# Routing logits from float16 halves, and the projection's bias added to the residual rows

## The chip, the cores and the metric

The kernel runs on one core of one Trainium2 chip. Its time is that of one execution on the device in microseconds; the median of three runs stands below. The engines are TensorE (PE in the profile, PEld for its weight loads), VectorE (DVE), ScalarE (ACT), GpSimd (POOL) and SyncE (SP, which here only issues DMAs).

## The reference

Cross-attention with tanh gate, then a mixture of experts with top-2 routing on the normalized rows, all in float32:

```python
def _L0_xattn_ref(q, k, v, w_qs, w_ks, w_vs, w_proj, b_proj):
    qh = jnp.einsum('bld,hdk->hblk', q, w_qs)
    kh = jnp.einsum('bld,hdk->hblk', k, w_ks)
    vh = jnp.einsum('bld,hdk->hblk', v, w_vs)
    attn = jax.nn.softmax(jnp.einsum('hblk,hbmk->hblm', qh, kh), axis=-1)
    out = jnp.einsum('hblm,hbmk->hblk', attn, vh) * qh
    out = out.transpose(1, 2, 0, 3).reshape(q.shape[0], q.shape[1], -1)
    return out @ w_proj.T + b_proj

def _L0_ffn_ref(x, gate_w, w1, w2):
    logits = jnp.einsum('td,ed->te', xt, gate_w)
    w_topk, sel = jax.lax.top_k(logits, K)
    w_topk = jax.nn.softmax(w_topk.astype(jnp.float32), axis=-1).astype(x.dtype)
    ...
    h = jax.nn.silu(jnp.einsum('td,edf->tef', xt, w1))
    y = jnp.einsum('tef,efd->ted', h, w2)
    out = jnp.einsum('ted,te->td', y, combine)

x = x + jnp.tanh(g_xattn[0]) * _L0_xattn_ref(_layernorm(x, axis=-1), ctx_1024, ctx_1024, ...)
x = x + jnp.tanh(g_ffn[0]) * _L0_ffn_ref(_layernorm(x, axis=-1), L0_ffn_gate_w, L0_ffn_w1, L0_ffn_w2)
```

x is 4 x 1024 rows of 256. There are 16 heads of 64, a context of 64 rows a batch, 8 experts with 1024 hidden columns, and K is 2. The bias b_proj is drawn with a spread of 0.1, so it is not zero.

## The kernel before

The kernel has two stages. `attention` (to about 380 us of the span) makes the attention, its residual sum, the routing, and writes each row twice, as a record per chosen expert, to DRAM. `experts` (the rest) works through 71 blocks of 128 records, with two products a block (L1372 and L1385), and adds the weighed results to the output.

Attention takes the 4096 rows in 8 groups of 512 (`NG`, `G`), a group as 4 tiles of 128 rows (`TG`). A group has 8 steps, one for each pair of heads (`p`). All engines run the same 64 steps and then a tail of 6, each in its own order written out by hand in a function `step`. They meet only through semaphores. A pair is worked on in a pipeline that is six steps deep: query product (L563), scores (L573) one step later, maximum and subtraction on DVE (L970, L975), exponent on ACT (L790), sum and reciprocal on DVE (L981, L984), the product with the reciprocal on POOL (`pn`, L1180), transposes on PE (L583), the product with v (L593), the product with q on DVE (`times_q`, r, L990), the rounding to float16 on ACT (`r_h`, L796), the rest on POOL (`r_l`, L1186), and the output product on PE (L608, L614), which sums over the eight pairs in the PSUM tile `pair_ps`. Products with a float32 meaning are made of three float16 products: high by high, high by low, low by high. A "high" half is the rounded value, a "low" half what the rounding left.

Other work is laid into fixed steps. In group g:
- step 1 and 2: the normalized rows of group g - 2 (in `rec`) are transposed by PE into `job_ps` in two halves (L622), and ACT copies each half to `x2t` in float32 (L802). In ACT's order the first copy is the first thing of step 2, right behind r_h of step 1; the second stands behind q's copy of step 2. Then PE makes the routing logits in float32 (`logits_products`, L161): 4 tiles by 2 halves of 128 with 8 columns each, which the trace shows as 16 instructions.
- step 3 and 4: DVE chooses the two experts of each row (`choose`, L188 to L201), in small instructions of 32 elements a partition, in a chain where each waits for the one before.
- step 4: PE makes the positions from the masks (`position_products`, 14 float16 products with 8 columns); step 5: DVE makes the record slots (`place`, L208 to L230), and POOL scatters the records, one a step.
- step 1 to 7: the first layer norm of group g + 1 (L903, L911, L914, L918, L716, L497, L725, L923). POOL makes the inverse root at step 3.
- step 6: DVE adds group g - 1's output product times tanh(g_xattn)/64 to its residual rows, `xres` (L996, `residual`). SP loads these rows from x at the start of their group. The statistics of the second layer norm follow at step 7.
- every step: an eighth of an expert's weights is split into halves by ACT (L830) and DVE (L1022).

The bias is part of the output product. ACT and DVE make `bias_rows`, whose row 0 holds the high half of 64 times the bias and whose row 32 the low half. With the last pair of a group PE multiplies `ones` with it, one product of 256 columns a tile (L611). The last pair of group g runs at step 5 of group g + 1, that of the last group in the tail.

## Time and profile before

| | us |
|---|---|
| median of 3 runs | 809.75 (808.73 to 811.44) |
| the profiled execution | 810.96 |
| its span | 809.2 |
| PE busy | 764.4 (94%) |
| DVE busy | 590.7 (73%) |
| POOL busy | 404.4 (50%) |
| ACT busy | 382.7 (47%) |

The span runs from the first to the last instruction; the execution's time has 1.8 us around it. Busy time is summed over both stages, and the stages differ: a share says little on which engine sets the pace of one of them. A timeline row gives an instruction's start and duration, both in us, and in brackets how long its engine had been idle before it and whom it waited for. An instruction can start before the one ahead of it on its engine has ended, so the distance between two starts is what an instruction costs its engine.

### The profile page before, as it was taken

The numbers are of one execution on the slowest core, as the hardware profiler recorded it, in microseconds if no ns is written. First come the engines' busy times: TensorE is split into PE (matmuls) and PEld (weight loads), VectorE is DVE, ScalarE is ACT, GpSimd is POOL, SyncE is SP. The second block draws the span as 40 slices with busy tenths as digits, with TensorE's granted clock in tenths as the row PEclk, the third lists the DMA queues.
The fourth block names the chain that finished last, engine by engine and source line by source line (L and its number), as shares of the span: only waits on it lengthen the run. The fifth ranks groups of instructions, "written<-read, shape, count | busy, mean of one in ns | idle before, by whom it ended". The sixth has DMA issues, their size and how long they took to land. (4 is left out here: it accounts for less than half of the span.)

```text
span 809.2 us, 22334 instructions
## 1 busy us (share of the span) xinstructions
PE 764.4 (94%) x7778; PEld 643.3 (79%) x7779; DVE 590.7 (73%) x1242; ACT 382.7 (47%) x688; POOL 404.4 (50%) x381
## 2 busy tenths in 40 slices
PE   3989999999999999997899989899999999999993
PEld 1656777777777777775899988899999999999993
DVE  7568798989898989795758668565665665666660
ACT  3565676666667666753345342233333333333230
POOL 5124444766665665664424657544434444444442
PEclk9999999999999999999899999999999999999997
DMA  7404151727263534422787854333233233222321
GB/s 263 183 1 156 45 191 59 261 73 263 77 217 123 186 122 157 158 105 79 235 229 213 240 145 110 62 47 51 47 46 50 46 47 48 49 46 47 52 28 20
DMA packets 48914, 92.61 MB, mean 114 GB/s; under 512 B 4936, under 2 KB 32656, under 8 KB 48848
## 3 DMA queue, kind: packets, MB, share of 16 engines
q1 hardware_dynamic: 25808, 64.84, 23.4%
q0 software_dynamic: 13392, 18.03, 12.8%
q10 hardware_dynamic: 9648, 8.85, 4.3%
q8 instruction: 41, 0.67, 0.4%
q14 instruction: 25, 0.20, 0.1%
HBM read 53.76 MB, written 37.95 MB: 113 GB/s over the span
## 5 line engine op out<-in xcount | busy, mean ns | idle before, releaser
L1372 PE MATMUL h_ps<-bx_h,w_now 128*128 128x128 f16 x2272 | 195.9, 220 | 0.6 <-DVE w_now L1508 0.6
L1385 PE MATMUL pair_ps<-weights,ht_h 128*128 x1136 | 190.3, 273 | 1.3 <-DVE ht_l L1516 0.8
L1372 PE MATMUL h_ps<-bx_l,w_now 128*128 128x128 f16 x1136 | 157.0, 220 | 0.0
L1372 PEld LDWEIGHTS h_ps<-bx_h,w_now 128*128 128x128 f16 x2272 | 154.4, 98 | 2.5 <-issue 1.2
L1385 PE MATMUL pair_ps<-weights,ht_l 128*128 x568 | 154.8, 273 | 0.0
L1444 ACT ACTIVATE hid<-h_ps 128x1024 f32<-128x1024 f32 x71 | 72.7, 1024 | 155.8 <-PE h_ps L1372 149.6
L1615 POOL TENSOR_TENSOR wait_mark<-wait_mark 128x1 f32<-128x1 f32 x71 | 44.6, 629 | 184.1 <-ACT y L1451 135.4
L1616 POOL DMA_INDIRECT out<-y,meta x71 | 124.7, 1757 | 17.9 <-issue 10.5
L1186 POOL TENSOR_TENSOR r_l<-r,r_h 128x512 f16<-128x512 f32 x64 | 74.3, 1161 | 110.9 <-ACT r_h L796 110.5
L1514 DVE CAST ht_h<-hid 128x1024 f16<-128x1024 f32 x71 | 49.5, 698 | 100.9 <-ACT hid L1444 100.3
L1385 PEld LDWEIGHTS pair_ps<-weights,ht_h 128*128 128x128 f16 x1136 | 110.1, 98 | 15.5 <-issue 1.8
L1508 DVE COPY w_now<-weights 128x4096 f16 x71 | 87.3, 1229 | 8.8 <-issue 2.9
L1516 DVE TENSOR_TENSOR ht_l<-hid,ht_h 128x1024 f16<-128x1024 f32 x71 | 87.0, 1226 | 2.4
L1372 PEld LDWEIGHTS h_ps<-bx_l,w_now 128*128 128x128 f16 x1136 | 88.0, 99 | 0.0
L1451 ACT ACTIVATE y<-pair_ps,meta 128x256 f32<-128x256 f32 x71 | 33.7, 474 | 107.5 <-DMA out<-y,meta 63.8
L1180 POOL TENSOR_TENSOR pn<-ex,rinv 128x512 f32<-128x512 f32 x64 | 66.5, 1038 | 35.0 <-DVE rinv L984 35.0
L573 PEld LDWEIGHTS s_ps<-kb,q 128*128 128x128 f32 x512 | 67.9, 193 | 8.6
L573 PE MATMUL s_ps<-kb,q 128*128 128x128 f32 x512 | 68.1, 276 | 0.0
L593 PE MATMUL ot_ps<-e,vb 128*128 128x512 f32 x128 | 65.6, 594 | 0.1
L608 PE MATMUL pair_ps<-wp_h,r_h 128*128 128x256 f16 x256 | 60.7, 273 | 0.1
L608 PE MATMUL pair_ps<-wp_l,r_h 128*128 128x256 f16 x256 | 60.7, 273 | 0.0
L1385 PEld LDWEIGHTS pair_ps<-weights,ht_l 128*128 128x128 f16 x568 | 55.6, 98 | 5.2
(258 smaller groups left out, 1351.8 us busy)
## 6 DMA issues: line engine op xcount, KB each, us to landing
stage<-in_w SPq DMA_DIRECT2D x16, 1024.0 KB, 8.1
w_split<-split SPq DMA_DIRECT2D x14, 1024.0 KB, 5.9
weights<-w_split SPq DMA_DIRECT2D x14, 1024.0 KB
rows<-records ACTq DMA_DIRECT2D x67, 129.0 KB
xin<-in_x SPq DMA_DIRECT2D x8, 512.0 KB, 5.7
x_even<-in_x SPq DMA_DIRECT2D x4, 512.0 KB
x_odd<-in_x SPq DMA_DIRECT2D x4, 512.0 KB
out<-x_even SPq DMA_DIRECT2D x4, 512.0 KB
```

The lines of the kernel that those rows point to most:

```text
L573: last = nc.tensor.matmul(s_ps[:, t].rearrange("p h m -> p (h m)"), q32[:, p, t * P:(t + 1) * P], kb[:, b, p, :] if isinstance(b, int) els ...
L593: nc.tensor.matmul(ot_ps[:, :], vb[:, b, p].rearrange("p h w -> p (h w)"), e32[:, p % 2, :], start=True, stop=True).then_inc(ot_mm, 1)
L608: nc.tensor.matmul(pj_ps[:, t, :], r_h[:, p % 2, t * P:(t + 1) * P], wt[:, p, :], start=(p == 0 and i == 0 and t % 2 == 0), stop=False, sk ...
L1180: nc.gpsimd.tensor_tensor(pn[:, p % 2].rearrange("p t (h m) -> p t h m", h=2), ex[:, p % 2].rearrange("p t (h m) -> p t h m", h=2), rinv[: ...
L1186: nc.gpsimd.tensor_tensor(r_l[:, p % 2, :], r32[:, p % 2, :], r_h[:, p % 2, :], ALU.subtract).then_inc(r_lo, 1)
L1372: last = nc.tensor.matmul(h_ps[r % 2][:, c, :], w1_now[:, r % 2, s, k * F + c * P:k * F + c * P + P], xt[:, r % 2, k, :], start=(j == 0 an ...
L1385: last = nc.tensor.matmul(y_ps[r % 2], ht[:, r % 2, c, :], weights_at(e, s, WN // 2 + c * D, D).rearrange("p o n -> p (o n)"), start=(c == ...
L1444: nc.scalar.activation(hid[:, r % 2], h_ps[r % 2][:, :, :], ACT.Silu, scale=1.0 / WS).then_inc(h_act, 1)
L1508: nc.vector.tensor_copy(w1_now[:, r % 2], weights[:, bass.ds(e, 1), :, 0:KD * F].rearrange("p o s n -> p (o s) n")).then_inc(w1_ready, 1)
L1514: nc.vector.tensor_copy(ht_h[:, r % 2], hid[:, r % 2]).then_inc(h_hi, 1)
L1516: nc.vector.tensor_tensor(ht_l[:, r % 2], hid[:, r % 2], ht_h[:, r % 2], ALU.subtract).then_inc(h_lo, 1)
L1616: pool.indirect_dma_start(out, bass.IndirectOffsetOnAxis(meta[:, r, 0:1].bitcast(U32), 0), y[:, r % 2, :], None, compute_op=ALU.add).then_ ...
```

## The change

The routing's normalized rows are kept as float16 halves instead of float32. ACT's two copies write the high halves. DVE gets a function `x2_split` that subtracts them from the PSUM tile and writes the low halves; it stands at steps 1 and 2, behind `times_q` and ahead of the expert split. The gate's weights are split once, in the setup. The logits are 24 products (4 tiles, 3 pairs of halves, 2 halves of the columns). PE's second transposes and its logits wait for DVE's subtractions (`x2_low`), where they waited for ACT's copies. The last two groups are routed in the expert stage, by the code as it was.

The bias leaves the output product. DVE makes tanh(g_xattn) times the bias once, in `tbias`, on all 128 partitions. POOL adds it to the residual rows in place (`add_bias`), 1024 elements a partition: for group g - 1 at the start of step 4 of group g, ahead of pn, and for the last group in the tail ahead of its fourth step. DVE's `residual` waits for POOL's sum in place of the load.

```diff
--- before.py
+++ after.py
+        carry.gate_hl = carried("gate_hl", [P, 2, KD, E], F16)
...
-    bias_rows = sb("bias_rows", [P, D], F16)
-    bias_high = sb("bias_high", [64, D], F16)
+    tbias = sb("tbias", [P, D], F32)
...
-    bias_sb = sb("bias_sb", [64, D], F32)
+    bias_sb = sb("bias_sb", [P, D], F32)
...
+    x2t_hl = x2t[:, :, :].rearrange("p k n -> p (k n)").bitcast(F16).rearrange("p (s k n) -> p s k n", s=2, k=KD)
...
+    biased = sem("biased")
+    gate_split, x2_low = sem("gate_split"), sem("x2_low")
...
-        sp.dma_start(bias_sb[:, :], dram["bproj"].partition_broadcast(64)).then_inc(bias_in, 16)
+        sp.dma_start(bias_sb[:, :], dram["bproj"].partition_broadcast(P)).then_inc(bias_in, 16)
...
-                pe.wait_ge(bias_hi, 2)
-                pe.wait_ge(bias_lo, 1)
...
@@ -607,8 +607,6 @@
 
                     nc.tensor.matmul(pj_ps[:, t, :], r_h[:, p % 2, t * P:(t + 1) * P], wt[:, p, :],
                                      start=(p == 0 and i == 0 and t % 2 == 0), stop=False, skip_group_check=True)
-                if p == NP - 1:
-                    nc.tensor.matmul(pj_ps[:, t, :], ones[:, :], bias_rows[:, :], start=False, stop=False, skip_group_check=True)
             pe.wait_ge(r_lo, n + 1)
...
         def logits(g):
-            pe.wait_ge(x2_copied, 2 * g + 2)
-            logits_products(nc, job_ps, x2t, gate_t).then_inc(routed.lg_mm, 1)
+            pe.wait_ge(x2_low, 2 * g + 2)
+            if g == 0:
+                pe.wait_ge(gate_split, 2)
+            for t in range(TG):
+                for i, (xs, gs) in enumerate(((0, 0), (0, 1), (1, 0))):
+                    for k in range(KD):
+                        last = nc.tensor.matmul(job_ps[:, t * E:(t + 1) * E], x2t_hl[:, xs, k, t * P:(t + 1) * P], carry.gate_hl[:, gs, k, :],
+                                                start=(i == 0 and k == 0), stop=(i == 2 and k == KD - 1))
+            last.then_inc(routed.lg_mm, 1)
...
             if p == 2 and known(g, 2):
-                pe.wait_ge(x2_copied, 2 * g - 3)
+                pe.wait_ge(x2_low, 2 * g - 3)
                 x2_transpose(g - 2, k, 1)
...
-        act.wait_ge(bias_in, 16)
-        nc.scalar.mul(bias_high[:, :], bias_sb[:, :], WS).then_inc(bias_hi, 1)
-        act.wait_ge(bias_zeroed, 1)
-        nc.scalar.mul(bias_rows[0:1, :], bias_sb[0:1, :], WS).then_inc(bias_hi, 1)
+        act.wait_ge(gate_copied, 1)
+        nc.scalar.copy(carry.gate_hl[:, 0], gate_t[:, :, :]).then_inc(gate_split, 1)
...
@@ -799,7 +802,7 @@
             act.wait_ge(x2_tp, 2 * g + k + 1)
             if k == 0:
                 after(act, routed.lg_mm, g)
-            nc.scalar.copy(x2t[:, k, :], job_ps[:, :]).then_inc(x2_copied, 1)
+            nc.scalar.copy(x2t_hl[:, 0, k, :], job_ps[:, :]).then_inc(x2_copied, 1)
...
-        nc.vector.memset(bias_rows[:, :].bitcast(U32), 0).then_inc(bias_zeroed, 1)
...
-        dve.wait_ge(bias_hi, 1)
-        dve.wait_ge(bias_zeroed, 1)
-        nc.vector.scalar_tensor_tensor(bias_rows[32:33, :], bias_sb[32:33, :], WS, bias_high[32:33, :],
-                                       ALU.mult, ALU.subtract).then_inc(bias_lo, 1)
+        dve.wait_ge(gate_split, 1)
+        nc.vector.tensor_tensor(carry.gate_hl[:, 1], gate_t[:, :, :], carry.gate_hl[:, 0], ALU.subtract).then_inc(gate_split, 1)
...
+        def x2_split(g, k):
+
+            dve.wait_ge(x2_copied, 2 * g + k + 1)
+            nc.vector.tensor_tensor(x2t_hl[:, 1, k, :], job_ps[:, :], x2t_hl[:, 0, k, :], ALU.subtract).then_inc(x2_low, 1)
...
         def residual(g, par):
 
             dve.wait_ge(pj_mm, pair_no(g, NP))
-            dve.wait_ge(xres_in[par], 16 * (g // 2) + 16 if isinstance(g, int) else g)
+            dve.wait_ge(biased, g + 1)
             nc.vector.scalar_tensor_tensor(xres[par][:, :, :], pj_ps[:, :, :], gains[:, 0:1], xres[par][:, :, :],
                                            ALU.mult, ALU.add).then_inc(x1_done, 1)
...
             if pairs_back >= 5:
                 times_q(n - 5, (p - 5) % NP)
+            if p in (1, 2) and known(g, 2):
+                x2_split(g - 2, p - 1)
             for i in pieces(g, p):
                 expert_lo(g, i)
...
                 dve.wait_ge(tanh_done, 1)
                 nc.vector.tensor_scalar(gains[:, :], tanhs[:, :], 1.0 / WS, None, ALU.mult).then_inc(setup_ops, 1)
                 dve.wait_ge(setup_ops, 1)
+                dve.wait_ge(bias_in, 16)
+                nc.vector.tensor_scalar(tbias[:, :], bias_sb[:, :], tanhs[:, 0:1], None, ALU.mult).then_inc(setup_ops, 1)
...
+        def add_bias(g, par):
+
+            pool.wait_ge(xres_in[par], 16 * (g // 2) + 16)
+            if g == 0:
+                pool.wait_ge(setup_ops, 2)
+            nc.gpsimd.tensor_tensor(xres[par][:, :, :], xres[par][:, :, :], tbias[:, :].unsqueeze(1).broadcast_to([P, TG, D]),
+                                    ALU.add).then_inc(biased, 1)
+
         def step(g, k, p, pairs_back=LAST):
             n = pair_no(g, p)
+            if p == 4 and known(g, 1):
+                add_bias(g - 1, 1 - k)
             if pairs_back >= 3:
                 normalize(n - 3, (p - 3) % NP)
...
         for p in range(LAST - 1):
+            if p == 3:
+                add_bias(NG - 1, 1)
             if p < 3:
                 normalize(NS + p - 3, NP + p - 3)
             product_lo(NS + p - 5, NP + p - 5)
```

## Rows read from the trace of the kernel before

**Rows 1.** The page, part 1: busy time of TensorE, share of span, instructions.
```profile
PE 764.4 (94%) x7778; PEld 643.3 (79%) x7779; DVE 590.7 (73%) x1242; ACT 382.7 (47%) x688; POOL 404.4 (50%) x381
```

**Rows 2.** Stretches: length, busy time (instructions) of each engine, clock, DMA share, GB/s.
```profile
core 0: us, PE busy (x) PEld busy (x) DVE busy (x) ACT busy (x) POOL busy (x), PEclk, DMA share, GB/s
...
157.50:200.40 42.90, 42.89 (x307) 31.99 (x306) 39.55 (x103) 29.31 (x56) 27.62 (x28) 1.00 0.47 163
```

**Rows 3.** Timeline of DVE, one group: start, duration, instruction, idle before, releaser.
```profile
164.57 0.69 DVE L1022 SCALAR_TENSOR_TENSOR split<-stage,split 128x512 f16<-128x512 f32 x1 [0.16 <-ACT split L830]
...
166.72 0.19 DVE L188 COPY lg<-job_ps 128x32 f32<-128x32 f32 x1 [0.62 <-PE job_ps L161]
...
168.99 0.69 DVE L970 TENSOR_REDUCE smax<-s_ps 128x8 f32<-128x512 f32 x1 [0.73 <-PE s_ps L573]
...
197.71 0.69 DVE L1022 SCALAR_TENSOR_TENSOR split<-stage,split 128x512 f16<-128x512 f32 x1 [0.69 <-ACT split L830]
```

**Rows 4.** Timeline of PE, same group: logits, positions and bias products.
```profile
164.83 1.85 PE L161 MATMUL job_ps<-gate_t,x2t 128*128 128x8 f32 x16
...
166.53 0.59 PE L563 MATMUL q_ps<-xt_h,wq_h 128*128 128x512 f16 x2
...
176.12 0.17 PE L170 MATMUL job_ps<-seen_h,ones 128*128 128x8 f16 x1
...
176.47 0.59 PE L563 MATMUL q_ps<-xt_h,wq_h 128*128 128x512 f16 x2
...
180.17 0.27 PE L611 MATMUL pair_ps<-bias_rows,ones 128*128 128x256 f16 x1
...
180.50 0.27 PE L611 MATMUL pair_ps<-bias_rows,ones 128*128 128x256 f16 x1
```

**Rows 5.** Timeline of DVE, step 6: the subtraction for xt_l and the next start.
```profile
185.23 0.64 DVE L923 TENSOR_TENSOR xt_l<-job_ps,xt_h 128x512 f16<-128x512 f32 x1
185.79 0.68 DVE L970 TENSOR_REDUCE smax<-s_ps 128x8 f32<-128x512 f32 x1
```

**Rows 6.** Timeline of DVE and ACT together, step 1.
```profile
158.84 0.68 DVE L990 TENSOR_TENSOR r<-ot_ps,q 128x512 f32<-128x512 f32 x1
...
159.56 0.62 ACT L796 CAST r_h<-r 128x512 f16<-128x512 f32 x1
...
159.60 0.69 DVE L1022 SCALAR_TENSOR_TENSOR split<-stage,split 128x512 f16<-128x512 f32 x1
...
160.08 0.58 ACT L802 COPY x2t<-job_ps 128x512 f32<-128x512 f32 x1
```

**Rows 7.** Timeline of POOL and DVE together, steps 3 and 4.
```profile
171.74 1.15 POOL L1186 TENSOR_TENSOR r_l<-r,r_h 128x512 f16<-128x512 f32 x1 [2.19 <-ACT r_h L796]
...
172.46 0.45 DVE L918 SCALAR_TENSOR_TENSOR shift<-mv,rstd 128x4 f32<-128x4 f32 x1
...
172.86 1.03 POOL L1180 TENSOR_TENSOR pn<-ex,rinv 128x512 f32<-128x512 f32 x1
...
173.04 0.90 DVE L192 TENSOR_TENSOR cand<-lg,top 128x32 f32<-128x32 f32 x1
```

**Rows 8.** Timeline of DVE and POOL together, step 3.
```profile
165.90 0.20 DVE L984 RECIPROCAL rinv<-esum 128x8 f32<-128x8 f32 x1
...
166.27 1.04 POOL L1180 TENSOR_TENSOR pn<-ex,rinv 128x512 f32<-128x512 f32 x1
...
167.16 0.19 DVE L192 TENSOR_TENSOR cand<-lg,top 128x32 f32<-128x32 f32 x1
```

**Rows 9.** Groups by line and form on POOL: busy time, mean ns, idle before.
```profile
L1194 POOL TENSOR_TENSOR wait_mark<-wait_mark 128x1 f32<-128x1 f32 x6 | 1.2, 195 | 6.7 <-DVE tok_ids L230 6.7
```

**Rows 10.** Timeline of DVE in the last group, step 4.
```profile
344.22 0.31 DVE L192 TENSOR_TENSOR cand<-lg,top 128x32 f32<-128x32 f32 x1
344.57 0.97 DVE L193 SCALAR_TENSOR_TENSOR cand<-cand,iota_e 128x32 f32<-128x32 f32 x1
```

**Rows 11.** Timeline of POOL in the tail.
```profile
376.43 1.16 POOL L1186 TENSOR_TENSOR r_l<-r,r_h 128x512 f16<-128x512 f32 x1 [2.19 <-ACT r_h L796]
```

More of the change, by code:

```diff
@@ L329, in attention @@
         "base_set", "consts_set", "k_zeroed", "v_zeroed", "wk_laid", "setup_ops", "tanh_done"))
-    ctx_tp, ctx_copied, gate_tp, gate_copied, wp_tp, wp_hi, wp_lo, wq_hi, wq_lo, bias_hi = (sem(n) for n in (
-        "ctx_tp", "ctx_copied", "gate_tp", "gate_copied", "wp_tp", "wp_hi", "wp_lo", "wq_hi", "wq_lo", "bias_hi"))
-    bias_zeroed, bias_lo = sem("bias_zeroed"), sem("bias_lo")
+    ctx_tp, ctx_copied, gate_tp, gate_copied, wp_tp, wp_hi, wp_lo, wq_hi, wq_lo = (sem(n) for n in (
+        "ctx_tp", "ctx_copied", "gate_tp", "gate_copied", "wp_tp", "wp_hi", "wp_lo", "wq_hi", "wq_lo"))
+    biased = sem("biased")
+    gate_split, x2_low = sem("gate_split"), sem("x2_low")
     k_mm, k_placed, v_mm, v_placed = (sem(n) for n in ("k_mm", "k_placed", "v_mm", "v_placed"))
```

## The prediction

> **What bounds the kernel now.** I read the page's busy line first: PE is busy for 94% of the span and DVE for 73% [rows 1]. That average hides two stages, so next came the table by stretches of one group, 42.90 us each. In the stretch shown PE is busy for 42.89 of 42.90 us and its clock is fully granted, so PE sets the pace of the attention stage. DVE is busy for 39.55 us, but its instructions start one right behind the other [rows 2]. The timeline of DVE shows how little room it has: in a whole group only four gaps carry a releaser, of 0.16 us (ACT's half of the expert split), 0.62 us (the logits), 0.73 us (the scores) and 0.69 us (again ACT's split) [rows 3]. That is 2.2 us of 42.90, so DVE is a second bound, 2.2 us behind the first. What the change gives to DVE has to fit in there.
>
> **The PE part.** A group's logits are 16 instructions that begin at 164.83 and end with the next product's start at 166.53: 1.70 us. The new form has 24 products of float16 halves with 8 columns. The nearest float16 products of that size are the 14 of the positions, from 176.12 to 176.47, so 0.025 us each and 24 cost 0.60 us [rows 4]. That saves 1.10 us in each of six groups, 6.6 us; the last two groups are routed in the expert stage by the old code. The bias products come one in three, 0.33 us between two of them, so 0.11 us each [rows 4]: four in each of eight groups, 3.5 us. Were PE the bound to the end, the change would win 6.6 + 3.0 us (the eighth group's bias lies in the tail, where the product waits for r_l anyway), 9.6 us. As bounds for a float16 product of 8 columns I take 0.025 and 0.11 us; at the upper end 24 of them cost 2.6 us and the logits lose 0.9 us a group.
>
> **The DVE part, step 1.** DVE gets two subtractions a group, each like the one that makes xt_l: next start 0.56 us after its own [rows 5]. The first stands at step 1 behind the product r (L990). It waits for ACT's copy of x2, and in ACT's order that copy stands behind the rounding of r to r_h, which waits for this same L990. In the trace L990 starts at 158.84 and ends at 159.52, r_h starts at 159.56, the copy at 160.08 and lasts 0.58 us to 160.66 [rows 6]. So the subtraction can't start before 160.70, and the expert split L1022, which started at 159.60, starts at 161.26: 1.66 us later. This wait is new, it comes in each of six groups, and behind it on DVE stand the sum of the exponents, on which POOL's pn hangs, and everything of step 2. PE's transposes of the second half wait for this subtraction too; I cost that at nothing, since PE has the query and score products of step 2 to do first. Bounds of the term: 0.6 us if ACT were far ahead (its order forbids that), 1.7 us as worked out. I take 1.66.
>
> **Step 2 and 3.** I walk DVE's starts against the old ones, both counted from the maximum of step 1, with which the stretch of rows 2 begins (157.5). At step 2 the second subtraction adds 0.56 us and the 0.16 us gap closes: L1022 at 8.87 instead of 7.04. The logits now wait for that subtraction, which ends at 8.95; before, they started at 7.30. PE idles 1.7 us there, has its logits at about 9.6 and gives back what it saved. DVE reads them at 10.3 instead of 9.2, because its own order reaches them only then. Next is a lock. DVE instructions with two inputs in SBUF stand still while POOL's tensor operations run: at step 4 L192 takes 0.90 us instead of 0.19, starting 0.18 us after pn and ending 0.04 us behind it; L918 ends just behind r_l in the same way [rows 7]. At step 3 today L192 starts at 167.16, when pn (166.27 to 167.31) is nearly through, and takes 0.19 us, since the logits came late enough [rows 8]. Changed, the logits are waiting already, so the copy, the maximum and L192 follow at once behind the reciprocal that lets pn start (165.90 in this group), with two starts of 0.22 us in between, and L192 is held until pn ends: 0.8 us more. The 0.73 us gap before the next maximum then closes. Maximum of step 3: 12.67 instead of 11.46, 1.2 us late.
>
> **Step 4: add_bias.** It stands on POOL ahead of pn and waits for nothing that is late (the residual rows land steps earlier), so it starts where pn starts now, right behind r_l. Its size is 1024 elements a partition. A 512-element POOL operation takes 1.04 us (pn) and 1.15 (r_l), one of a single element 0.195 us [rows 7, 9], so twice the part that grows gives 1.9 to 2.1; I take 2.0, with 1.04 (pn as it is) and 2.3 us (r_l twice) as ends. L192 is held to its end, and pn follows back to back. In the last group this case is already in the trace: L192 slips in at the end of r_l and the next instruction, L193, is held 0.97 us by pn [rows 10]. So DVE waits for add_bias and for pn: 2.0 us more, less the 0.2 us that L193 takes anyway. That is 1.9 us; the maximum of step 4 comes at 20.4 instead of 17.3, and DVE is 3.1 us late. PE's positions wait for the masks and idle some 2 us more. If the lock did not bite, this term would be zero, since POOL's idle time hides it (2.19 us before the r_l of this step [rows 7]) and pn is needed one PE step later.
>
> **Steps 5 to 0.** DVE runs here without a gap until ACT's split at step 0, and that gap stays, since ACT's chain starts from DVE's L990 of step 7. So a group's period becomes 42.9 + 3.07 = 45.96 us. PE stands idle for 4.5 us of it.
>
> **A price from a page.** The rows make add_bias 2.0 us [rows 7, 9]. The Trainium skill, page GPSIMD Engine Reference, section 2.1 (Instruction dispatch), gives about 2.5 cycles an element for two inputs, with a clock of 1.2 GHz; an estimate from that page is 1024 x 2.5 cycles = 2.1 us and the fixed 0.2 us: 2.3 us, and the time would be 1.7 us above my forecast.
>
> **The sum.** Group 1 gains its bias products, 0.4 us, for PE still has the pace there. Five periods lie between step 1 of group 2 and step 1 of group 7: 5 x 3.07 = 15.4 us. Group 7 prepares no next group, so DVE has no statistics to make there and waits for PE at steps 1 and 2 today; PE comes into it some 1 us ahead, and by the same walk DVE is 0.5 us early at step 3. Step 4 makes it 1.6 us later (L192 finds a gap there, L193 and the next one are held [rows 10]), and DVE's waits of steps 6 and 7 take back about 0.5: I count +0.5 us. In the tail add_bias runs in front of the last but one r_l, where POOL waits 2.19 us for ACT [rows 11]: hidden, and if longer, 0.1 to 0.3 us. The setup (a bias load twice as wide, one small split, tanh times bias, against two ACT and one DVE instruction removed) I cost at 0, within 0.5: DVE waits for PE in group 1 and takes it up. The expert stage only moves. Sum: -0.4 + 15.4 + 0.5 = +15.4 us. The profiled execution took 810.96 us (809.2 span and 1.8 around it), 1.2 us above the median of the runs: 826.4 for such an execution, 825.2 against the median. I forecast 825 us.
>
> **Rivals.** (1) PE keeps the pace and the win shows: 809.75 - 9.6 = 800 us. For it speaks PE's 42.89 us; against it DVE's 2.2 us of room, of which the first wait alone takes 1.66. (2) The locks don't add up: add_bias is short for DVE, or L192 gets in first. Then step 3 ends 0.6 us late and ACT's gap at step 0 takes a little: 0.5 us a group, 5 x 0.5 - 0.4 = +2, 812 us. Against it stand 0.90 and 0.97 us in the rows. (3) DVE loses more: add_bias at 2.3 us and L1022, which also has two SBUF inputs, now meeting r_l of POOL at step 1 or 2 for up to 0.4 us each. That is 0.7 to 1 us a group, 5 x 0.9 = 4.5: 830 us. It decides from the point where r_l starts before L1022 ends.
>
> **Chances.** Forecast (820 to 829) 0.60, between it and rival 2 (locks in part) 0.13, rival 2 0.10, rival 3 0.08, rival 1 0.09. So the range of 8 in 10 is 811 to 831. About 0.3%, 2.4 us, is what a measurement can tell. Faster by more: rival 1, 0.09. Within: 0.05, the lower part of rival 2. Slower: 0.86.
>
> **What would show it.** In the changed profile a group's period is 46 us and DVE has no gap for scores or logits; a gap of some 1.2 us stands before the x2 subtraction of step 1, released by ACT's copy; the logits' product waits for DVE, the positions for the mask; PE is busy about 41.4 us of 46 (42.9 less 1.1 and 0.4). L192 takes some 2 us at step 4 and L193 1 us, and 1 us at step 3. I am wrong if L192 stays short while add_bias runs, if add_bias is under 1.5 us, or if the period is below 43.

## The result, and the profile after

The changed kernel takes 827.97 us (median of 4 runs, 825.25 to 828.93) and the kernel before, on the same chip, 809.24 us (4 runs, 807.85 to 811.44): a ratio of 1.0223, with a 95% interval of 1.0189 to 1.0258. It is slower, by 18.7 us. The profiled execution took 828.93 us, its span is 827.2 us against 809.2.

Where the 18.0 us of span lie, read from starts of the same instruction in both timelines (after less before):

| stretch | before | after | added |
|---|---|---|---|
| to the maximum of step 1 of group 2 | 114.63 | 115.85 | +1.22 |
| from there to step 1 of group 7 | 213.50 | 231.35 | +17.85 |
| from there to the tail's maximum (group 7) | 35.91 | 36.82 | +0.91 |
| from there to the last attention product | 15.66 | 16.68 | +1.02 |
| from there to the end | 429.5 | 426.5 | -3.0 |

Almost all of it is in the five periods of the attention stage: 46.27 us each instead of 42.70 (in the middle of the stage, 42.90). The last row is the expert stage, which the change doesn't touch. From its last copy of the logits to the end of the span, where all kernels of this document have the same code, the profiled executions took 345.9 to 352.8 us (350.2 before, 348.8 after), so 3 us there are no effect that can be told from that spread.

The page of the kernel after, parts 1 and 2, answers to [rows 1]:

```profile
span 827.2 us, 22385 instructions
## 1 busy us (share of the span) xinstructions
PE 766.9 (93%) x7794; PEld 636.0 (77%) x7795; DVE 615.6 (74%) x1254; ACT 379.9 (46%) x687; POOL 426.9 (52%) x389
...
PEclk9989999999999999999899999999999999999998
```

Three whole periods after, cut where DVE copies the logits, and three slices of 2 us, each just behind a group's logits (length; busy time and count of PE, PEld, DVE, ACT and POOL; granted clock; DMA share; GB/s). They answer to [rows 2]:

```profile
173.02:218.82 45.80, 42.47 (x312) 30.10 (x311) 43.13 (x106) 28.98 (x54) 30.29 (x29) 1.00 0.44 150
218.82:265.70 46.88, 44.10 (x312) 31.37 (x311) 43.11 (x105) 28.93 (x54) 30.28 (x29) 0.96 0.42 147
265.70:311.51 45.81, 42.46 (x310) 30.05 (x309) 43.14 (x105) 28.97 (x54) 30.30 (x29) 0.99 0.43 150
...
219.00:221.00 2.00, 2.00 (x8) 1.46 (x7) 1.83 (x6) 0.60 (x1) 2.00 (x3) 0.50 0.72 193
...
266.00:268.00 2.00, 2.00 (x16) 1.71 (x14) 1.79 (x7) 0.75 (x2) 1.98 (x2) 1.00 0.75 256
...
312.00:314.00 2.00, 2.00 (x8) 1.36 (x7) 1.59 (x5) 0.49 (x1) 1.80 (x3) 0.50 0.76 246
```

PE is no longer busy throughout: 42.5 of 45.8 us, where it was 42.89 of 42.90. DVE has gone from 39.55 to 43.1 us and sets the pace. And there are two kinds of period, 45.8 and 46.9 us; in the longer one the granted clock is 0.96 over the period and 0.50 in the slice just behind the logits. The clock falls behind the first, the third and the fifth of the six logits (from 126, 218 and 311 us). The third of these falls lies in the last period, 45.71 us, which is shorter by itself, since group 7 prepares no next group: without a fall it is 44.50 us (see the spare products).

DVE's timeline of one group after (start, duration, instruction, idle before and what ended it), from two groups of rows, answers to [rows 3, 7, 8]:

```profile
165.88 0.69 DVE L965 TENSOR_TENSOR x2t<-job_ps,x2t 128x512 f16<-128x512 f32 x1 [1.17 <-ACT x2t L805]
...
173.02 0.14 DVE L189 COPY lg<-job_ps 128x32 f32<-128x32 f32 x1
...
173.42 0.92 DVE L193 TENSOR_TENSOR cand<-lg,top 128x32 f32<-128x32 f32 x1
...
179.33 2.21 DVE L193 TENSOR_TENSOR cand<-lg,top 128x32 f32<-128x32 f32 x1
181.58 0.97 DVE L194 SCALAR_TENSOR_TENSOR cand<-cand,iota_e 128x32 f32<-128x32 f32 x1
```

POOL's timeline over the same step, and in the tail (this answers to [rows 7, 11]):

```profile
179.14 2.35 POOL L1213 TENSOR_TENSOR x_even<-x_even,tbias 128x1024 f32<-128x1024 f32 x1
181.46 1.04 POOL L1189 TENSOR_TENSOR pn<-ex,rinv 128x512 f32<-128x512 f32 x1
...
394.17 2.54 POOL L1213 TENSOR_TENSOR x_odd<-x_odd,tbias 128x1024 f32<-128x1024 f32 x1
396.67 1.16 POOL L1195 TENSOR_TENSOR r_l<-r,r_h 128x512 f16<-128x512 f32 x1
```

Read the two together: L193 starts at 179.33, 0.19 us behind the start of add_bias, and ends at 181.54; add_bias ends at 181.49. L194 starts 0.12 us behind pn and ends at 182.55; pn ends at 182.50. A comparison of 32 elements, 0.19 us by itself, ends when the POOL instruction ends under which it started.

PE's timeline: the logits' product of two groups, and the products behind it in the second (answers to [rows 4]):

```profile
171.73 0.76 PE L630 MATMUL job_ps<-gate_hl,x2t 128*128 128x8 f16 x24 [1.54 <-DVE x2t L965]
172.34 0.59 PE L565 MATMUL q_ps<-xt_h,wq_h 128*128 128x512 f16 x2
...
217.52 0.76 PE L630 MATMUL job_ps<-gate_hl,x2t 128*128 128x8 f16 x24 [1.54 <-DVE x2t L965]
218.14 0.59 PE L565 MATMUL q_ps<-xt_h,wq_h 128*128 128x512 f16 x2
218.57 0.82 PE L565 MATMUL q_ps<-xt_l,wq_h 128*128 128x512 f16 x2
219.18 1.06 PE L565 MATMUL q_ps<-xt_h,wq_l 128*128 128x512 f16 x2
220.03 1.91 PE L575 MATMUL s_ps<-kb,q 128*128 128x128 f32 x8
```

The 24 products take 0.61 us (171.73 to 172.34), so they are as cheap as they were to be. But PE now stands 1.54 us in front of them, and in the second group a pair of 512-column products that takes 0.59 us at full clock takes 1.06 behind that wait: the clock is at its lower level, 1.2 instead of 2.4 GHz.

### The profile page after: what moved, and what is told of

Same layout as the page of the kernel before. It is cut to its first block and busy times, and to the rows that moved or that the text cites. A ratio compares the mean times of both kernels' runs of the same rounds, so it can differ in the third digit from the quotient of the medians.

```text
span 827.2 us, 22385 instructions
## 1 busy us (share of the span) xinstructions
PE 766.9 (93%) x7794; PEld 636.0 (77%) x7795; DVE 615.6 (74%) x1254; ACT 379.9 (46%) x687; POOL 426.9 (52%) x389
## 5 line engine op out<-in xcount | busy, mean ns | idle before, releaser
L1465 ACT ACTIVATE hid<-h_ps 128x1024 f32<-128x1024 f32 x71 | 72.7, 1024 | 155.9 <-PE h_ps L1393 148.4
L1636 POOL TENSOR_TENSOR wait_mark<-wait_mark 128x1 f32<-128x1 f32 x71 | 47.9, 675 | 182.5 <-ACT y L1472 134.0
L1637 POOL DMA_INDIRECT out<-y,meta x71 | 121.7, 1714 | 16.5 <-issue 9.1
L1195 POOL TENSOR_TENSOR r_l<-r,r_h 128x512 f16<-128x512 f32 x64 | 76.1, 1190 | 101.3 <-ACT r_h L799 101.3
L1189 POOL TENSOR_TENSOR pn<-ex,rinv 128x512 f32<-128x512 f32 x64 | 66.6, 1040 | 45.1 <-DVE rinv L989 45.1
L575 PEld LDWEIGHTS s_ps<-kb,q 128*128 128x128 f32 x512 | 69.5, 200 | 14.4 <-issue 7.5
L575 PE MATMUL s_ps<-kb,q 128*128 128x128 f32 x512 | 71.3, 284 | 2.7 <-DVE ssub L980 2.7
L799 ACT CAST r_h<-r 128x512 f16<-128x512 f32 x64 | 39.4, 616 | 72.0 <-DVE r L995 71.7
```

What stands on the lines that cost most here:

```text
L575: last = nc.tensor.matmul(s_ps[:, t].rearrange("p h m -> p (h m)"), q32[:, p, t * P:(t + 1) * P], kb[:, b, p, :] if isinstance(b, int) els ...
L1189: nc.gpsimd.tensor_tensor(pn[:, p % 2].rearrange("p t (h m) -> p t h m", h=2), ex[:, p % 2].rearrange("p t (h m) -> p t h m", h=2), rinv[: ...
L1195: nc.gpsimd.tensor_tensor(r_l[:, p % 2, :], r32[:, p % 2, :], r_h[:, p % 2, :], ALU.subtract).then_inc(r_lo, 1)
L1465: nc.scalar.activation(hid[:, r % 2], h_ps[r % 2][:, :, :], ACT.Silu, scale=1.0 / WS).then_inc(h_act, 1)
L1637: pool.indirect_dma_start(out, bass.IndirectOffsetOnAxis(meta[:, r, 0:1].bitcast(U32), 0), y[:, r % 2, :], None, compute_op=ALU.add).then_ ...
```

## The experiments

My theory after the result: the loss is DVE's, in two parts that add up. The bias part costs through the hold of choose()'s two-input instructions by add_bias at step 4; the logits part through the wait for ACT's half at step 1 and the hold at step 3. The rivals: POOL's longer work delays its own results; PE's clock, which falls behind the new wait, is the main part; one of the two edits does nothing. "Period" is the distance between two copies of the logits by DVE (L189 after, L188 before) in the middle of the stage, so the last of the five, shorter in most kernels, is left out; each ratio is to the kernel before, timed on the same chip in the same session.

| kernel | median us | ratio (95% interval) | period us |
|---|---|---|---|
| before | 809.2 to 809.9 | 1 | 42.90 |
| after | 827.97 | 1.0223 (1.0189 to 1.0258) | 45.8 / 46.9 |
| logits only | 815.34 | 1.0071 (1.0039 to 1.0104) | 43.7 / 45.2 |
| bias only | 821.22 | 1.0148 (1.0119 to 1.0176) | 44.69 |
| after, bias at step 6 | 812.80 | 1.0060 (1.0028 to 1.0093) | 43.8 / 45.1 |
| after, half of the bias | 819.79 | 1.0139 (1.0109 to 1.0168) | 44.70 |
| after, choose() through PSUM | 813.65 | 1.0058 (1.0036 to 1.0079) | 43.4 / 45.1 |
| bias only, at step 6 | 808.06 | 0.9989 (0.9957 to 1.0020) | 42.80 |
| step 6 and PSUM | 816.93 | 1.0080 (1.0056 to 1.0105) | 43.4 / 45.1 |
| step 6, PSUM, split later | 804.48 | 0.9938 (0.9911 to 0.9964) | 42.83 |
| after, split later | 824.89 | 1.0201 (1.0165 to 1.0236) | 45.18 |
| step 6, PSUM, spare products | 809.86 | 1.0000 (0.9975 to 1.0025) | 43.44 |
| after, spare products | 824.42 | 1.0179 (1.0143 to 1.0214) | 45.78 |
| step 6, split later | 808.50 | 0.9990 (0.9963 to 1.0017) | 43.16 |

**Logits only.** The kernel before with the float16 logits; the bias stays a product.

> The kernel before with the float16 logits alone; the bias stays in the output product. My theory (the new wait of the logits on ACT's and DVE's halves moves DVE's r = ot*q of step 1, and through it GpSimd's r_l, onto choose()'s two-input instruction of step 3, but nothing is added to the lock of step 4): DVE ends some 1 to 1.3 us late a group, of which the period takes 0.9 to 1.3, so 809.5 + 5 x 1.1 = about 815 (812 to 818), and the lock at step 3 is 0.9 us as in the kernel after. Rival A, GpSimd's add_bias has no part in the loss and the logits alone do it all: 828, with the logits 45.8 us or more apart. Rival B, the products saved on PE pay for the wait: 803 to 806.

Measured: 815.34 us, periods of 43.70 and 45.19 us in turn. The total is the theory's, but partly by luck. The 43.70 is +0.80, just below the 0.9 to 1.3 us that DVE's walk gives; the periods of 45.19 I had not expected, and they are not DVE's: the granted clock is 0.50 behind the logits with which they begin (see the spare products below).

**Bias only.** The kernel before with add_bias at step 4.

> The kernel before with the bias part alone: add_bias of 2.35 us on GpSimd in step 4, the float32 logits as they were. My theory (DVE is held at choose()'s two-input instruction of step 4 by add_bias, about 2.2 us where it was about 0.3 held before, and has some 2.2 us of waits a group to give up before it sets the period, while PE saves 0.11 us at each of four bias products): the period stays within -0.4 to +0.5 us of 42.9, so 807 to 812, with the waits of DVE for PE gone in the rest of the group. Rival, the lock doesn't matter and the period is PE's: 42.9 - 0.44, so 806. Rival 2, both parts simply add and this one is worth 2 us a group: 819.

Measured: 821.22 us, outside my range and nearest to the second rival: the parts nearly add (0.71% and 1.48% make 2.19%, and both together cost 2.23%; by the periods without a fall of the clock, 0.80 and 1.79 us make 2.59, and both together cost 2.90). DVE's timeline of one group:

```profile
168.29 0.19 DVE L188 COPY lg<-job_ps 128x32 f32<-128x32 f32 x1 [0.62 <-PE job_ps L161]
...
170.56 0.69 DVE L956 TENSOR_REDUCE smax<-s_ps 128x8 f32<-128x512 f32 x1 [0.73 <-PE s_ps L572]
...
174.62 2.21 DVE L192 TENSOR_TENSOR cand<-lg,top 128x32 f32<-128x32 f32 x1
176.86 0.97 DVE L193 SCALAR_TENSOR_TENSOR cand<-cand,iota_e 128x32 f32<-128x32 f32 x1
```

The hold is as forecast: L192 and L193 take 3.18 us where they took 1.09 [rows 7], 2.09 more. But the waits of 0.62 and 0.73 us are still there, unchanged. They were never room. DVE's lag of step 4 reaches PE (its positions now wait 0.78 us for the masks, and later scores 0.42 us for DVE), PE comes as much later to the next group's logits, which take it 1.7 us, and DVE waits for them again as before. Only ACT's gap gives something back: 0.86 us a group before, 0.58 now. 2.09 less 0.28 is 1.81, and the period grew by 1.79.

**The bias at step 6.** The same work on POOL at step 6 of the group's own walk: two steps later within the period, and six steps earlier for the group whose rows it is. The call in the tail falls away with it (its removal isn't shown):

```
-            if p == 4 and known(g, 1):
-                add_bias(g - 1, 1 - k)
+            if p == 4 and isinstance(g, int) and g == 1:
+                add_bias(0, 0)
+            if p == 6 and known(g, 1):
+                add_bias(g, k)
```

> The kernel after, but GpSimd adds the bias to a group's rows two steps later, at step 6 of the group's own walk, where DVE has no two-input instruction of choose() in flight. Same work in all. My theory (the place of add_bias, not its length, costs): the 2.2 us hold at step 4 goes to 0.3 or less, some of it comes back where DVE's r = ot*q meets the busy port, and the period falls from 46.3 to 43.7 to 44.5: 812 to 818. Rival, the loss is GpSimd's or PE's clock and not the hold: 826 to 830, unchanged.

> The bias part alone (float32 logits), with add_bias at step 6. The bias part alone at step 4 gave 821 and a period of 44.69 us with every logits wait as before. My theory (the hold on choose() is all of that loss): the 2.21 and 0.97 us instructions go back to 0.90 and 0.19, the period to 42.9 less what PE's saved bias products give, 0 to 0.44: 806 to 810. Rival, GpSimd's longer work delays its r_l or pn and PE with them wherever it stands: 813 or more.

Measured: 812.80 us with both parts and 808.06 with the bias part alone, each inside my range. With the bias part alone the period falls from 44.69 to 42.80 us by the move. In its timelines add_bias is as long as ever, and the two instructions of step 4 are back at the lengths of [rows 7]:

```profile
170.47 0.90 DVE L192 TENSOR_TENSOR cand<-lg,top 128x32 f32<-128x32 f32 x1
171.40 0.19 DVE L193 SCALAR_TENSOR_TENSOR cand<-cand,iota_e 128x32 f32<-128x32 f32 x1
```

```profile
181.99 2.36 POOL L1192 TENSOR_TENSOR x_odd<-x_odd,tbias 128x1024 f32<-128x1024 f32 x1
```

So the place of add_bias cost 1.9 us a group, and its 2.36 us of POOL's time cost nothing. The saved bias products are worth 0.1 us a period (42.80 against 42.90), not 0.44. The rest stays at step 6: PE's transposes of xn begin 0.70 us behind the product ahead of them instead of 0.44, just after ACT has made xn, and take 0.09 us more.

**Half of the bias.** add_bias over half of the tiles; half of the bias is left out.

> The kernel after with add_bias on half of the tiles of each group, 512 elements instead of 1024 in each partition: it leaves half of the bias out. My theory (each microsecond of add_bias is a microsecond of DVE's hold at step 4 and so of the period, since DVE has no room left): the instruction takes 1.18 us, the hold falls by as much, the period by 1.1, and five periods and the tail give 828 - 6 = 822 (820 to 824). Rival, only that an instruction stands there matters, or the clock: 827 to 829.

Measured: 819.79 us, just below the range. The instruction takes 1.26 to 1.31 us, the comparison is held for nearly as long, and the period is 44.70, 1.1 us below the 45.80. The clock falls only once, in its first period (45.77), and three times in the kernel after: over all five periods it is 7.8 us shorter, 5.5 by the hold and the rest by the two falls fewer. DVE and POOL:

```profile
218.85 1.12 DVE L193 TENSOR_TENSOR cand<-lg,top 128x32 f32<-128x32 f32 x1
220.01 0.96 DVE L194 SCALAR_TENSOR_TENSOR cand<-cand,iota_e 128x32 f32<-128x32 f32 x1
```

```profile
L1213 POOL TENSOR_TENSOR x_odd<-x_odd,tbias 128x512 f32<-128x512 f32 x4 | 5.2, 1310 | 0.0
L1213 POOL TENSOR_TENSOR x_even<-x_even,tbias 128x512 f32<-128x512 f32 x4 | 5.0, 1260 | 0.0
```

1.09 us less of hold, 1.1 us less of period: while DVE sets the pace, each microsecond of the hold is one of the period.

**choose() through PSUM.** add_bias stays at step 4, but cand, choice, the second maximum and the copy of the logits that choose() reads lie in unused PSUM columns, so that none of its instructions has two SBUF inputs:

```
+    def spare(i, n=TG * E):
+        return job_ps[:, 128 + 64 * i:128 + 64 * i + n]
...
+        cand, choice, lg = by_tile(spare(0)), spare(1, TG), by_tile(job_ps[:, 0:TG * E])
+        if c:
+            top = spare(2, TG)
...
+        mask = by_tile(spare(3))
+        nc.vector.tensor_tensor(mask, carry.iota_e[:, :, :], over_e(choice), ALU.is_equal)
```

> The kernel after, with add_bias where it is, but choose() keeps cand, choice, the second maximum and the first copy of the logits in spare PSUM columns, so that none of its instructions reads two SBUF operands on DVE (one comparison is done twice for it). My theory (DVE's instructions with two SBUF inputs wait for GpSimd's running tensor_tensor, others don't): the 0.92, 2.22 and 0.97 us instructions of steps 3 and 4 fall to 0.2 each, DVE gets 3.3 us a group back, the period falls from 46.3 to 43 to 43.8 where PE's own work and the logits' wait take over, 809 to 814. Rival A, it is GpSimd's traffic itself that slows any DVE instruction: 828 or worse. Rival B, the hold only moves to the next instruction with two SBUF inputs (split of the expert weights in step 4): about 818 to 822.

Measured: 813.65 us, inside the range. POOL's add_bias still takes 2.35 us and still starts in front of the comparison (174.63 and 174.82), and no instruction of choose() is held. The grouped rows of DVE, all groups (busy us, mean ns, idle before), where L204 and L205 are the comparison and the one behind it:

```profile
L205 DVE SCALAR_TENSOR_TENSOR job_ps<-job_ps,iota_e 128x32 f32<-128x32 f32 x12 | 2.4, 199 | 0.4
...
L204 DVE TENSOR_TENSOR job_ps<-job_ps,top 128x32 f32<-128x32 f32 x6 | 1.2, 200 | 0.2
L204 DVE TENSOR_TENSOR job_ps<-lg,job_ps 128x32 f32<-128x32 f32 x6 | 1.2, 196 | 0.2
```

In the kernel after, the same two have means of 1422 and 689 ns:

```profile
L193 DVE TENSOR_TENSOR cand<-lg,top 128x32 f32<-128x32 f32 x12 | 17.1, 1422 | 0.4
L194 DVE SCALAR_TENSOR_TENSOR cand<-cand,iota_e 128x32 f32<-128x32 f32 x12 | 8.3, 689 | 0.4
```

This shows the mechanism and not only its place: it is the second SBUF operand that makes DVE stand, not POOL's activity. The periods of 45.1 in this kernel, three of the four in the middle, are falls of PE's clock again. The Trainium skill, page SBUF — State Buffer, section "SBUF: two separate sides", says the same: between a DVE instruction with two SBUF inputs and a GpSimd one that reads SBUF, the one that starts first has the port pair for its whole length. The trace agrees: 2.21 us of hold under a 2.35 us instruction, 0.20 us once an operand is in PSUM.

**Both of these.** The kernel after with add_bias at step 6 and choose() through PSUM.

> The kernel after with both: add_bias at step 6 and choose() through PSUM. From the kernel with add_bias at step 6 (812.8, periods 43.8 and 45.1) this takes the last holds of choose(), 0.73 and 0.71 us at steps 3 and 4. If DVE is still the bound, the period falls by 1.1 to 1.4 (one comparison more): 806 to 808. Rival, the half clock that PE falls to behind its logits wait in every second group sets the period: those stay at 45.1 and the time at 812.

Measured: 816.93 us, not 806 to 808, and above the rival's 812 too; the profiled execution took 812.94. Three of its five periods are 45.1 us, as the rival said, the others 43.4 and 42.1; DVE now waits 2.8 to 4.4 us a group and is no bound. What is? In PE's timeline and in slices of 2 us around the logits:

```profile
255.76 0.76 PE L645 MATMUL job_ps<-gate_hl,x2t 128*128 128x8 f16 x24 [1.54 <-DVE x2t L980]
256.38 0.93 PE L580 MATMUL q_ps<-xt_h,wq_h 128*128 128x512 f16 x2
257.10 1.06 PE L580 MATMUL q_ps<-xt_l,wq_h 128*128 128x512 f16 x2
```

```profile
254.00:256.00 2.00, 0.46 (x12) 0.25 (x11) 2.00 (x4) 0.86 (x2) 0.47 (x2) 1.00 0.18 66
256.00:258.00 2.00, 2.00 (x26) 0.98 (x23) 1.83 (x8) 0.70 (x1) 2.00 (x2) 0.62 0.07 20
258.00:260.00 2.00, 2.00 (x9) 1.64 (x8) 0.49 (x3) 0.60 (x1) 1.80 (x3) 0.52 0.93 344
```

PE did 0.46 us of work in the slice ahead, and then its clock is at 0.62 and 0.52. The other groups have the same wait, and behind two of the five the clock stays up.

**Spare products.** To part the clock from the wait: PE runs three products whose result is overwritten, ahead of the wait. Once in that kernel, once in the kernel after.

```
         def logits(g, n, par):
+            after(pe, q_sb, n)
+            for _ in range(3):
+                nc.tensor.matmul(q_ps[1][:, :], wq_h[:, 0, 3 * P:4 * P], xt_h[:, par, 0, :], start=True, stop=True)
             pe.wait_ge(x2_low, 2 * g + 2)
```

> The kernel with add_bias at step 6 and choose() through PSUM (periods 43.4 and 45.1 in turn), and PE runs three spare 128x512 float16 products of about 0.22 us each into the bank that the next q product overwrites, ahead of the logits' wait. Their result is not used. They fill 0.65 of the 1.54 us wait with work and leave what the kernel waits for as it was. My theory (the long periods are PE's clock falling behind that wait): the granted clock stays at 1.00, every period is 43.4 to 43.5, the time 807 to 812 beside 813 to 817 without. Rival, the long periods come from something else, a DMA or the order of events in two groups: 43.4 and 45.1 still in turn, 813 to 817.

> The kernel after with the same three spare products on PE ahead of the logits' wait and nothing else. My theory: no fall of the granted clock in the groups, periods of 45.8 only, 828 less two or three times 1.08 = 825 (824 to 827): the clock is the smaller part of the loss and DVE sets the 45.8. Rival, the clock is the main part: 820 or less.

Measured: 809.86 us against 816.93 without (on another chip; the kernel before took 809.9 and 809.2 there), with four periods of 43.44 and a last one of 42.17; 824.42 us against 827.97, with four periods of 45.76 to 45.79 and a last one of 44.50. Both as the theory had it. The logits start behind DVE as before, PE's idle ahead of them is 0.90 us instead of 1.54, and the clock stays up. Over its five periods the kernel after gets 3.45 us back, 1.1 to 1.2 for each of its three falls; the medians say 3.55. The same places in the first of the two:

```profile
207.61 0.76 PE L649 MATMUL job_ps<-gate_hl,x2t 128*128 128x8 f16 x24 [0.90 <-DVE x2t L984]
208.22 0.59 PE L580 MATMUL q_ps<-xt_h,wq_h 128*128 128x512 f16 x2
```

```profile
207.00:209.00 2.00, 1.39 (x28) 1.01 (x29) 1.97 (x5) 1.56 (x2) 1.30 (x1) 1.00 0.04 12
209.00:211.00 2.00, 2.00 (x17) 1.77 (x15) 1.52 (x8) 0.60 (x1) 2.00 (x3) 1.00 0.66 170
```

**The split later.** DVE's first x2_split stands behind the expert split of step 1 instead of in front of it. In the kernel after alone, with add_bias at step 6, and with both other edits:

```
-            if p in (1, 2) and known(g, 2):
-                x2_split(g - 2, p - 1)
+            if p == 2 and known(g, 2):
+                x2_split(g - 2, 1)
             for i in pieces(g, p):
                 expert_lo(g, i)
+            if p == 1 and known(g, 2):
+                x2_split(g - 2, 0)
```

> The kernel after with one change of order: DVE's first x2_split (step 1) stands behind the expert split of that step, not in front. My theory (the 1.17 us wait of DVE for ACT's half is on the bound chain, and PE's 1.54 us wait ahead of the logits, which the same wait causes, is what lets its clock fall in every second group): DVE waits 0.4 us instead of 1.17, PE 0.9 instead of 1.54, the period falls from 45.8 to 45.0 and the longer ones of 46.9 are gone: 828 - 5 x 1.25 = 821 to 823. Rival, the logits wait for the second split and DVE's wait is slack: 827 to 829.

> The kernel after with add_bias at step 6 and the first x2_split behind the expert split, but choose() as it was. From 812.8 (periods 43.8 and 45.1): DVE gets 0.78 us of its wait back and the clock stays up, so the period is 42.9 to 43.0 throughout and the time 805 to 808. Against the version with choose() through PSUM (804.5, period 42.83) it tells what that part still gives: my theory, under 1 us. Rival, DVE's holds of 0.73 and 0.71 us in choose() still set the period: 43.5 or more, 809 to 811.

> The same as the kernel with add_bias at step 6 and choose() through PSUM, and DVE's first x2_split (step 1) stands behind the expert split of that step instead of in front, so that the 1.17 us wait for ACT's half is filled with 0.68 us of work. My theory: another 0.6 us of DVE's time a group, unless PE has become the bound at about 41.5 to 42.4 us: 801 to 806, faster than the kernel before. Rival, nothing gained because the logits product waits for the second split, not the first: as without it, 806 to 808.

Measured: 824.89 us, 808.50 us and 804.48 us. The first is 2 us above my range by its median, though its period, 45.18, is near what the theory gives (45.0) and its profiled execution took 820.12; the other two are 0.5 us above the range and inside it. The times of these kernels spread by more than their periods do, for two reasons that the profiles show: the expert stage (345.9 to 352.8 us, as above), and the granted clock from 52 to 61 us, in the first group, which is 1.00, 0.81 or 0.65 in executions of the same setup. So I read the mechanisms from the periods. DVE's wait is 0.39 us instead of 1.17, PE's 0.94 instead of 1.54, and no period is a long one. In the last of them PE has the clock throughout and neither engine is full:

```profile
166.99:209.82 42.83, 41.77 (x312) 30.44 (x311) 39.70 (x107) 29.36 (x54) 30.48 (x29) 1.00 0.48 161
...
251.35 0.76 PE L645 MATMUL job_ps<-gate_hl,x2t 128*128 128x8 f16 x24 [0.94 <-DVE x2t L980]
```

(A row of the stretches and one of PE's timeline.) It is faster than both kernels: 0.9938 of the kernel before, interval 0.9911 to 0.9964 (its profiled execution was the slowest of its 12, 810.28, with a clock of 0.81 from 52 to 61 us and the 352.8 us of expert stage). With choose() left as it was, the period is 0.33 us longer, 1.7 us over five where I expected under 1, and the ratio of 0.9990 can't be told from 1. The period of 42.83 hardly differs from the 42.90 of before, and all five together are 1.2 us shorter (213.27 against 214.50), so most of the 4.7 us that the fastest one gains in its median isn't in the five periods; where it is stays open.

## Why the prediction was right, point by point

The forecast was 825 us, slower; it took 827.97. By its steps:

- **The new float16 products cost 0.60 us.** Right: 0.61 us for 24. **PE's savings of 9.6 us don't show.** Right, since PE waits 1.54 us in front of the logits and 1.26 in front of the positions. It stands idle for less than forecast, 3.3 us of a period and not 4.5, and the bias products alone would have won 0.1 us a period and not 0.44.
- **Step 1: the expert split starts 1.66 us later.** Right. Counted from the maximum of step 1 it was forecast for 3.73 us; it starts at 166.49, 3.77 us behind 162.72. The new wait is 1.17 us in the trace.
- **Step 2: the logits start at 8.95 us.** Right: 171.73 is 9.01 behind the same mark.
- **Step 3: L192 is held 0.8 us more, and the maximum comes 1.2 us late.** Right: 0.92 us instead of 0.19, and 12.55 us (175.27) where the forecast was 12.67.
- **Step 4: add_bias takes 2.0 us and DVE loses 1.9.** The mechanism is right, the term was mis-sized: 2.35 us, and the two held instructions take 3.18 us instead of 1.09, a loss of 2.09. The rows from which I scaled (1.04 and 1.15 us for 512 elements) gave too little; 1.26 us for 512 and 2.35 for 1024 elements say that a sum of two float32 operands grows by 1.09 us for each 512. The estimate that I drew from the Trainium skill, page GPSIMD Engine Reference, section 2.1 (Instruction dispatch), 2.3 us, was the better one.
- **A period of 45.96 us.** The undisturbed ones are 45.8: DVE's busy time up by 3.6 us (43.13 against 39.55) and its idle time down by 0.7 (2.67 against 3.35), so 2.9. Of the 3.6, 2.8 are the holds and the rest is mostly the two subtractions, 0.6 us each from start to start, less what others lost (the sum at L914 takes 0.81 us instead of 0.97). ACT's gap at step 0, which was to stay, went from 0.69 to 0.41 us.
- **Not in the forecast at all: PE's clock.** It fell in three of the five periods, behind the logits' wait: 46.86, 46.88 and the last, 45.71 us. With the spare products these are 45.76, 45.77 and 44.50, together 3.4 us, and the medians differ by 3.55.
- **The setup within 0.5 us of zero.** The row came out at +1.2 (with group 1 in it, for which -0.4 was forecast), but not by the change. By 52 us the kernel after was 0.75 us ahead; then the stretch from 52 to 61 us has a mean granted clock of 0.65 instead of 0.81. Three other kernels of this document have its setup, and in group 1 differ from it by half an add_bias at most; their first copy of the logits by DVE comes at 124.70 us with a clock of 0.81 (spare products), 122.06 and 121.76 with 1.00 (half of the bias, split later), and in the kernel after at 126.16 with 0.65. With the spare products, at the 0.81 that the kernel before had, the mark of the table's first row comes at 114.39, 0.24 us early: the forecast held. What sets the clock there stays open.
- **Group 7 costs 0.5 us, the tail 0.1 to 0.3.** They cost 0.9 and 1.0, each more than forecast. In the tail add_bias takes 2.54 us and r_l follows it back to back at 396.67, so the 2.19 us of idle [rows 11] didn't hide it: the stretch is 16.68 us with the bias part alone too, and 15.56 to 15.66 with half of the bias, with add_bias at step 6 and with the logits alone.
- **The expert stage only moves.** It came out 3.0 us shorter, within what it differs by from one execution to the next; without it the time would have been 831.

So the number was near for two reasons. The DVE walk was right to 0.2 us at each step. The other is luck: measured less forecast is +1.6 us up to group 2, +2.45 for the five periods (17.85 against 15.4), +0.4 for group 7 and +1.0 for the tail, together 5.5, against -3.0 in the expert stage. The +2.45 hides two misses. The falls of the clock, which the forecast doesn't have, are 3.4 us; without them the kernel with the spare products needs 14.4 us more than the kernel before for the same stretch, and the walk had put 1.0 us too much on it.

**The rivals.** (1), PE keeps the pace, 800 us, and (2), the holds don't add up, 812 us, are refuted: PE waits in front of the logits and the positions, and half of the bias takes as much off the period as off the hold. (3), 830 us, came near in its time but not by its reason: add_bias was as long as it said, but the expert split was not held by r_l; it is 0.68 us long at both steps.

One reason in the prediction was wrong without harm to the number. I called DVE's 2.2 us of gaps room into which the change has to fit. The bias part alone showed that 1.35 us of it, the waits for the logits and the scores, comes back however late DVE is. In the full change those waits did close, and with the logits alone too, where in the period of 43.70 us DVE waits only for ACT: the float16 logits had taken 1.1 us off PE at that very place. With the bias part alone I trusted the room, and missed by 9 us.

## What to carry to other kernels

Before work goes to GpSimd, look at which DVE instruction starts while it runs: one with two SBUF inputs, however small, is held to its end, and here 2.35 us of free GpSimd time cost 1.8 us a group at one place and nothing two steps later. A wait in the trace is room only if the engine waited for doesn't itself come later when you are late: follow it once round the loop. And a new wait on TensorE can cost twice, by itself and by the clock that falls behind it; filling it with spare products gave back the clock, and moving the work that it waits for by one instruction gave back the clock and 0.6 us of the wait.

## What the hardware did that I had not expected

- Behind a wait of PE of 1.54 us ahead of the logits the granted clock fell to one half in three of five groups (the kernel after); behind one of 0.90 or 0.94 us at the same place it never fell in the middle of the attention stage, in five kernels. It isn't the wait alone: of the kernels with the 1.54 us, the one with half of the bias had one fall in five groups and the one with choose() through PSUM had four. What decides between two groups with the same wait I did not part.
- The fall costs 1.1 us where DVE sets the pace (46.9 against 45.8) and 1.65 us where DVE has 2.8 us of waits in a group (45.08 against 43.43).
- The first group's stretch from 52 to 61 us, behind a wait of PE of 2.90 us, has a granted clock of 1.00, 0.81 or 0.65 in executions of the same setup; with it the first copy of the logits comes at 121.8 to 126.2 us. What decides between them is open.
- What GpSimd adds in front of pn at step 4 is passed on to DVE whole (1.09 us less of add_bias, 1.09 less of hold), and pn itself then holds the next two-input instruction for another 0.97 us.
